# Residual and router logits out of one widened output projection, with the choice of experts spread over four slots, in an attention and mixture-of-experts kernel

## The reference, cut to what matters

```python
x = x + xattn(layernorm(x), ctx, Wq, Wkv, Wc)      # y @ Wc.T ends the attention
xf = layernorm(x)                                  # per token
logits = xf @ router_w.T                           # 8 numbers per token
top_vals, top_idx = top_k(logits, 2)
probs = softmax(top_vals)
for e in range(8):
    w = sum(where(top_idx == e, probs, 0))
    h = gelu(xf @ w1[e].T + b1[e])                 # 128 -> 512
    out += w * (h @ w2[e].T + b2[e])               # 512 -> 128
x = x + out
```

## Time and profile before

| | |
|---|---|
| runs | 418.19, 419.75, 419.78 us; median 419.75 us |
| the profiled execution's own time | 418.32 us |
| its span, first to last instruction | 416.4 us |
| mean granted TensorE clock | 0.912 of 2.4 GHz |
| busy: PE, DVE, ACT, POOL | 325.8, 269.5, 226.4, 241.2 us |
| DMA | 62.95 MB, 151 GB/s on average |

### The profile page before, as it was taken

One profiled execution on the slowest core, in us unless ns is written; L12 is line 12 of the kernel. 1 busy time (PEld: TensorE's weight loads), 2 busy tenths in 40 slices (PEclk: granted clock), 3 DMA queues, 4 the chain that ended last, 5 costly groups with the idle time before them and its releaser, 6 DMA issues.

```text
span 416.4 us, 11632 instructions
## 1 busy us (share of the span) xinstructions
PE 325.8 (78%) x3716; PEld 262.4 (63%) x3716; DVE 269.5 (65%) x846; ACT 226.4 (54%) x533; POOL 241.2 (58%) x384
## 2 busy tenths in 40 slices
PE   2635869998989898877987079975997999999850
PEld 0213346666656565655765069965986999999840
DVE  8225887977879788778757337644676455556652
ACT  1321557787858677565655036633554566666630
POOL 7786425342426757474667606884788565576550
PEclk9999889999989989898769569996999999999995
DMA  4599442674534625311111266671665776668945
GB/s 140 124 223 248 131 116 84 132 161 123 168 99 128 169 69 144 104 50 49 37 44 39 88 200 184 171 245 51 194 182 152 238 241 213 192 217 256 323 143 176
DMA packets 57114, 62.95 MB, mean 151 GB/s; under 512 B 14109, under 2 KB 40116, under 8 KB 56896
## 3 DMA queue, kind: packets, MB, share of 16 engines
q1 hardware_dynamic: 50432, 50.34, 43.5%
q0 software_dynamic: 4320, 8.47, 5.9%
q10 hardware_dynamic: 2304, 3.41, 2.7%
HBM read 37.65 MB, written 11.88 MB: 119 GB/s over the span
## 4 chain that ended last, share of the span: by engine, by line
PE 54%; DVE 13%; POOL 8%; SPq 8%; issue 7%; ACT 5%; DMA 5%; DVEq 0%; POOLq 0%; ACTq 0%
PE sexp L1227 11%; PE smax L1218 11%; PE smax L1015 7%; PE tail L1059 7%; DVE shift L1314 4%; PE feed L1006 3%; SPq L443 3%; POOL dispatch_d L693 2%; DMA stacks<-dispatch_d 2%; POOL result_d L782 2%; PE sexp L1023 2%; PE feed L1094 2%; PE heads L1069 2%; PE prep L1077 2%; PE feed L1001 1%
## 5 line engine op out<-in xcount | busy, mean ns | idle before, releaser
L1314 DVE TENSOR_REDUCE shift<-smax 128x4 f32<-128x512 f32 x128 | 86.3, 683 | 38.6 <-PE smax L1015 37.5
L782 POOL DMA_INDIRECT result_d<-y_out,stacks x71 | 70.7, 996 | 29.4 <-issue 26.5
L855 ACT ACTIVATE probs<-sexp 128x512 f32<-128x512 f32 x128 | 73.8, 593 | 23.9 <-PE sexp L1023 23.0
L1227 PE MATMUL sexp<-w_sb,probs 128*128 x568 | 77.8, 281 | 9.4 <-ACT probs L952 9.3
L1218 PE MATMUL smax<-probs,w_ring 128*128 128x128 f32 x568 | 78.6, 283 | 1.5 <-ACT probs L948 1.0
L1227 PEld LDWEIGHTS sexp<-w_sb,probs 128*128 128x128 f32 x568 | 70.3, 195 | 11.8 <-issue 11.5
L693 POOL DMA_INDIRECT dispatch_d<-rows_out,row_i x64 | 62.8, 981 | 24.2 <-issue 13.0
L1783 DVE TENSOR_TENSOR probs<-smax,b_cols 128x512 f32<-128x512 f32 x71 | 49.1, 691 | 41.9 <-PE smax L1218 38.2
L1218 PEld LDWEIGHTS smax<-probs,w_ring 128*128 128x128 f32 x568 | 71.5, 198 | 2.8 <-issue 2.3
L952 ACT ACTIVATE probs<-probs 128x512 f32<-128x512 f32 x71 | 44.8, 630 | 45.8 <-DVE probs L1783 44.8
L1015 PE MATMUL smax<-stacks 64*128 64x128 bf16 x512 | 52.2, 231 | 21.2 <-DVE shift L1314 9.3
(11 more groups left out here) (214 smaller groups left out, 516.1 us busy)
## 6 DMA issues: line engine op xcount, KB each, us to landing
w_ring<-w_t_dram SPq DMA_DIRECT2D x71, 256.0 KB, 3.4
stacks<-kpart SPq DMA_DIRECT2D x48, 128.0 KB
stacks<-qpart SPq DMA_DIRECT2D x48, 128.0 KB
stacks<-dispatch_d SPq DMA_DIRECT2D x71, 65.0 KB, 3.2
stacks<-result_d ACTq DMA_DIRECT2D x12, 256.0 KB, 4.5
ctx<-ctx_t_dram SPq DMA_DIRECT2D x8, 256.0 KB, 3.5
w_sb<-w_t_dram SPq DMA_DIRECT2D x8, 256.0 KB, 3.4
out_dram<-xs SPq DMA_DIRECT2D x8, 256.0 KB, 3.3
```

Source lines behind the costliest of these rows:

```text
L782: nc.gpsimd.indirect_dma_start(out=result_d, out_offset=bass.IndirectOffsetOnAxis(ap=xg[r][:, D + 1:D + 2].bitcast(U32), axis=0), in_=y_ou ...
L855: nc.scalar.activation(dst, sexp[hp][:], ACT.Exp).then_inc(exp_done, 1)
L1227: last = nc.tensor.matmul(down_ps[i], hidden[i][:, c * P:(c + 1) * P], w2_sb[:].rearrange("p e c d -> p (e c d)")[:, bass.ds(e * FF + c * ...
L1314: nc.vector.tensor_reduce(shift4[n % 2][:, hp, 0, 4 * m:4 * m + 4], smax[hp][:], AX.X, ALU.max, negate=True).then_inc(max_taken, 1)
```

## The change

Identity and router are put beside each other in one tile of 136 columns (`ident_wide` = identity and centred router), and Wc beside the product of Wc and the centred router (`wc_wide`). `project_y` now accumulates two products in PSUM: the turned x of the batch times `ident_wide`, and y times `wc_wide`. The result is the new x and, in 8 more columns, the router's logits, short of the factor 1/std, which does not change their order and goes into the gap of the two best later (`scale_gap`). The sum is copied by ScalarE to `xw`, of which `xs` and `logits` are views (`xs` has now a stride of 136 words). Four turns of x for a group (`turn_x`) and a copy (`copy_xt`) take the place of `turn_rows`, `copy_normed` and `project_router`.

The moments are `bn_aggr`, one for each batch. Routing has eight rounds of 4, each with 20 steps, which stand between other work over the four slots 9+4r to 12+4r (and a fifth for the shares). Sends are spread 1, 2, 3, 2 over four slots; round 6 is sent in one run ahead of stage 2, and round 7 is chosen there (`route_last`) and sent at every third tile from 8 on. `table_first` is in slots 33 to 35, `table_second` at tiles 6 to 15, and the rows of padding are stored one at a time at tiles 24 to 31.

```diff
-ROUNDS = (0, 4, 8, 12, 16, 20, 24, 28, 31, 32)
-TURN_AT = (12, 16, 20, 24, 27, 31, 35)
-RANK_AT = (16, 20, 24, 27, 29, 33)
...
+ROUND = BATCH // GB
+ROUTE_AT = 2 * GB + 1
+SENDS = {1: 1, 2: 2, 3: 3, 4: 2}
+SENDS_LAST = {0: 3, 1: 3, 2: 2}
+PADS_AT = 24
+LAST_SENDS_AT = 8
-        xs = sb("xs", [P, BATCH, D])
+        xw = sb("xw", [P, BATCH, WIDE])
+        xs = xw[:, :, 0:D]
+        logits = xw[:, :, D:WIDE]
...
# PE
+            def turn_x(g, n):
+                pe.wait_ge(y_ready, n)
+                for b in range(GB):
+                    last = nc.tensor.transpose(heads[:, b * SEQ:(b + 1) * SEQ], xs[:, GB * g + b, :], ident)
+                last.then_inc(xt_turned, 1)
...
-                nc.tensor.matmul(prep[:, 0:D], y_t[:], wc_sb[:], start=True, stop=True).then_inc(proj_done, 1)
+                pe.wait_ge(xt_copied, n // GB + 1)
+                nc.tensor.matmul(proj_ps, x_t[:, n % GB * SEQ:(n % GB + 1) * SEQ], ident_wide[:], start=True, stop=False)
+                nc.tensor.matmul(proj_ps, y_t[:], wc_wide[:], start=False, stop=True).then_inc(proj_done, 1)
# ACT
+            def copy_xt(g):
+                act.wait_ge(xt_turned, g + 1)
+                if g:
+                    act.wait_ge(proj_done, GB * g)
+                nc.scalar.activation(x_t[:], heads[:], ACT.Copy).then_inc(xt_copied, 1)
+            def residual(n):
+                act.wait_ge(proj_done, n + 1)
+                nc.scalar.activation(xw[:, n, :], proj_ps, ACT.Copy).then_inc(resid_done, 1)
# POOL
+            for _ in range(TOPK * GB):
+                send_next(FIRST_ROUNDS)
+            row_scale(ROUND - 1)
+            place_rows(ROUND - 1)
+            scale_gap(ROUND - 1)
+            share_ratio(ROUND - 1)
             def between(t):
...
+                n, off = divmod(t - LAST_SENDS_AT, 3)
+                if off == 0 and 0 <= n < TOPK * GB:
+                    send_next(ROUND - 1)
# DVE, after the slots
+            def between(t):
+                r = ROUND - 1
+                if t == 1:
+                    norm_rows(r)
+                if t == 2:
+                    row_ranks(r)
+                    row_terms(r)
+                if t == 3:
+                    row_numbers(r)
+                    row_indices(r)
+                if t == 4:
+                    share_sum(r)
+                    share_first(r)
+                    share_second(r)
+                if 6 <= t < 16:
+                    table_second(t - 6)
# SP
-            sp.wait_ge(sexp_done, UNITS * BATCH)
+            sp.wait_ge(sexp_done, UNITS * FIRST_BATCHES)
...
-                if t == FIRST - BULK:
-                    store_pads()
+                if PADS_AT <= t < PADS_AT + EXPERTS:
+                    store_pad(pads[t - PADS_AT])
```

More of the change, by code:

```diff
@@ L368, in batches @@
         def batches(r):
-            return slice(ROUNDS[r], ROUNDS[r + 1])
-        def many(r):
-            return ROUNDS[r + 1] - ROUNDS[r]
+            return slice(GB * r, GB * (r + 1))
         def rows_gone(eng, r):
-            eng.wait_ge(rows_sent[r % RR], 16 * TOPK * sum(many(q) for q in range(r % RR, r + 1, RR)))
+            eng.wait_ge(rows_sent[r % RR], 16 * TOPK * GB * (r // RR + 1))
         def feeding(s, lag):
@@ new lines, in _ @@
+                n = 0
+                for lag, count in SENDS.items():
+                    r = routing(s, 3 + lag)
+                    if r is not None and r < FIRST_ROUNDS - 1:
+                        for _ in range(count):
+                            n += 1
+                            if n > 1:
+                                pace(s, n)
+                            send_next(r)
+                if s - LAST_SLOT + len(SENDS_LAST) > 0:
+                    for _ in range(SENDS_LAST[s - LAST_SLOT + len(SENDS_LAST) - 1]):
+                        send_next(FIRST_ROUNDS - 1)
@@ L789, in _ @@
                 between(t)
-            assert all(sent[r] == TOPK * many(r) for r in range(ROUND))
+            assert all(sent[r] == TOPK * GB for r in range(ROUND))
         @block.scalar
@@ L922, in _ @@
                     split_q_rest(g)
+                r = routing(s, 3)
+                if r is not None:
+                    norm_row(r, 3)
                 if 0 <= e < BATCH:
                     exp(e, 1)
+                if turning(s) is not None:
+                    copy_xt(turning(s))
                 if 0 <= a < BATCH:
@@ L1569, in _ @@
                     assert consts[0] == PAD_CONSTS
+                r = routing(s, 4)
+                late = r is not None and r < FIRST_ROUNDS - 1
+                if late:
+                    row_indices(r)
+                r = routing(s, 2)
+                if r is not None:
+                    mark_number(r, 1)
+                r = routing(s, 1)
+                if r is not None:
+                    choose(r, 0)
                 g = feeding(s, 4)
```

687 lines of the change are left out of this document (303 added, 384 removed), and 3 rows, old and new, of the table SEND_COUNT.

## The result

The changed kernel takes 385.22 us (the median of 383.85, 385.06, 385.37 and 463.06), the kernel before 418.97 in the same comparison. The ratio is 0.924, with a 95% interval of 0.918 to 0.929. Forecast were 389.6 us and a range of 379.0 to 404.5. The profiled execution took 385.06 us with a span of 383.3: 33.1 us less than the span before, where the sum of the prediction has 28.7.

A forecast was written before the change was run, and what follows sets the result against it. Stage 1 was taken to go at the pace of TensorE and VectorE together, stage 2 of TensorE alone. Terms +1.5 + 2.0 - 3.6 - 11.0 - 4.4 - 13.5 + 0.3 = -28.7 from 418.3 gave 389.6 us, range 379 to 404.5.

The forecast's parts named there:

- Start: Up to batch 4: added small products, turns and copies, x loaded in 512 B pieces and wider projections cost +1.5 us.
- Batches 4 to 8: Stage 1 before routing: a second product per projection and turning x with its wait cost +2.0 us.
- Batches 8 to 20: Stage 1 with routing and projections: router step and lower clock go, wider projection adds; 21.6 us per four, -3.6 us.
- Batches 20 to 28: Stage 1 after projections end: at full clock 19.5 us for each four in place of 25.0, -11.0 us.
- the router step shows why: Stage 1's low clock: TensorE waits 1.21 us, does 1.06 us of tiny products, then attend takes 1.93 instead of 1.08.
- Batches 28 to 31: Last three batches of stage 1, 11.4 us: claimed to stay as they are.
- Between the stages: Last attend to first tile's turn: table ends at 6.5 us instead of 10.9, turn at +14.0 instead of +18.5; -4.4 us.
- Stage 2: Waits for ratio, padding and table, low clock and router work go, 14.5 us; about 1.0 comes back; -13.5 us.
- The slots keep their pace: Rival, stage 1: four maxima and exps set the pace, TensorE's savings become idle time; 404.2 us, chance 0.18.
- The clock stays high: Rival, batches 8 to 28: clock stays high and waits vanish, 19.9 and 17.7 us per four; 379.4 us, chance 0.12.
- the slower case: Rival, stage 1: TensorE waits for ScalarE's late copy of the sum, 2.3 us in 21 slots; 438 us, chance 0.05.
- the rule on the emptied pipe: VectorE's pipe empties after each operation, waiting or not: 20 steps save 0.7 us, not 2; sum some 2.5 us longer.

## Why the prediction was right, point by point

- **Start (+1.5, measured +0.5).** x in pieces of 512 B lands later, 8.0 us for the 1 MB in place of 6.4, and nobody waits for it. The term was too large, and near what the start varies by: the first attend of the same code lies at 53.6 us in one trace and at 52.6 in the other. The Trainium skill, DMA: Bandwidth & Descriptors, "Why small descriptors are slow (HBM only)", has the direction right: small pieces are slower, and this load took 1.6 us longer.
- **Batches 4 to 8 (+2.0, measured +2.0), right by accident.** The prediction puts 1.0 on the second product and 1.0 on the turns of x and their wait. With the ranks and the turns moved, all of that costs 0.3 us net. What makes the 2 us is the count of ranks of round 0, which the change puts into this stretch and which brings a wait of its own, 1.3 us. The prediction did not name this wait.
- **Batches 8 to 20 (-3.6, measured -4.4).** The step is right and shown from both sides: with the stall put back the clock is 0.93 again, and with the stall taken out of the kernel before it is 1.00. The size of the clock's part is too large: 1.6 us was read from one four at 0.93, and the whole stretch has 0.95, with 1.00 behind the first step. 21.3 us for each four, forecast 21.6. Its other half also holds: spread steps cost 0.10 us, bunched ones 0.22, and bunching them costs 3.4 us in the first round.
- **Batches 20 to 28 (-11.0, measured -13.4): the term that was mis-sized**, and 2.4 of the 4.4 us that the sum lacks. TensorE's own work is as worked out: 16.2 us for four batches, forecast 16.4. I added 1.3 us for VectorE's and GpSimd's share and 1.6 of waits, from the batches 4 to 8, and rounded 19.3 up to 19.5; measured are 18.3 us, so 2.1 of waits in all. That the other engines have room with no projections in these slots is my reading, not a test. The forecast also took both fours for like the last one, 24.7 us at 0.78. The first is another case, 25.4 us at 0.93 with two rounds' router steps in it, at 167.0 and 185.0 us. It lost 7.4 us, the last one 6.0, where 5.5 were forecast for each. And in the last one the clock had fallen to 0.57 at a place with no router step close ahead of it, so "the router step shows why" is only part of the cause there.
- **Batches 28 to 31 (0, measured -0.5).** I let them stand, though the clock of the kernel before was 0.74 there; it is 1.00 now.
- **Between the stages (-4.4, measured -4.1).** The table ends 6.6 us after the last attend, forecast 6.5. Two errors cancel: SP waits 1.5 us for the sends of round 5, named as the next to be late but held to be in time, and the tile lands 1.1 us faster, since the weights went ahead.
- **Stage 2 (-13.5, measured -13.5).** The holes are gone, and GpSimd's run of eight sends is just covered, as said: the ratio ends 23.7 us after the attend, forecast 21.5. VectorE starts the rows of round 7 0.2 us after their offsets, and the first result is 0.7 us late, which nothing waits for. The 1.0 us that comes back is 0.5 and 0.9 before the tiles 10 and 16, where the table has 1.0 and 2.0 us of steps at one tile. But the prices inside the term are not what I took them for: spacing the sends alone brought 3.2 of the 7.3 us, and the padding's gain was there without the spreading. That the total fits to the tenth is luck.
- **The rivals.** "The slots keep their pace" is out: all groups of four behind batch 8 are shorter. "The clock stays high" came true for the clock; its time of 379.4 asks for waits to vanish too, and they did not. ScalarE's copy of the sum, the slower case, is not waited for in a single slot. The time of 385 lies between forecast and fast rival.
- **Two figures beside the sum.** By the rule on the emptied pipe the 20 steps save 1.3 us less for each four, which is 7.8 us of VectorE's time over six groups; the 2.5 that the prediction puts on it is not derived from a row. GpSimd, put at 18.8 of 21.6 us, is busy 46.5 of 64.0 in the batches 8 to 20, 15.5 for each four.

## What to carry to other kernels

A wait on TensorE can have two prices, its own length and the work behind it at half the clock; here a wait of 1.2 us ahead of 1 us of tiny products cost 3.7 us, and the same products 1.25 once another product covered the wait. Ask first whether the stalled step can stand behind the next independent matmul: that alone gave about 2% of the kernel before. Put long chains of small steps between steps of other work, and price a move by the run that undoes it, since two terms of this sum were right only in total.

## What the runs showed of the hardware that I had not expected

- A stall of 1.21 us and 1.06 us of 128x8 products are enough for TensorE to fall to its lower level in a stretch that has none of it otherwise: attend in 1.50 and 1.94 us, clock 0.93 over 24.7 us. With a wait of 0.20 us ahead of the same products it stays at 1.00, and so it does with a wait of 1.27 us and the count of ranks behind it.
- It is no rule: behind a wait of 1.30 us with the same kind of products attend took 1.08 us once, and stretches of 6.9 and 6.4 us without such products ahead of them had a clock of 0.57 (behind waits of 0.92, 0.38, 0.28 and 0.56 us) and 0.59 (behind 1.47 and 1.5).
- Eight stores by SP with row numbers from one load took 4.5 us, in the kernel before with one load for each 8.24.
- A tile of 65 KB landed in 2.05 us when the weights had been issued 3 us ahead, and in 3.2 to 3.3 us when they had been issued 1.5 us ahead.
- The kernel before took 418 to 420 us on some chips, 450 and 450 to 456 us on two others. In the traces of its variants and those of the changed kernel on these two, the difference came as waits of 2 to 5 us, in stage 1 most of them once in a round, not as a slower pace of every instruction: the batches 4 to 11 took the same time. The cause is open, and the kernel before itself has no trace there.
